# SiLU on the gate half and normalising chunk by chunk in a two-layer sequence kernel with routed experts

## What is computed

```python
scores = softmax(xt @ Wr)
topk_w, topk_idx = top_k(scores, 2)               # 8 experts, 2 for each token
topk_w = topk_w / (topk_w.sum(-1) + 1e-20)
g = silu(einsum('th,ehd->etd', xt, Wg)); u = einsum('th,ehd->etd', xt, Wu)
out = sum over the two chosen experts of topk_w * ((g * u) @ Wd)
shared = silu(x @ Sg) * (x @ Su) @ Sd
x = layernorm(x + out + shared)
```

## Time and profile before

| | |
|---|---|
| median of 3 runs | 1100.16 us (1098.81 to 1102.42) |
| the profiled execution: its own time | 1101.61 us |
| its span | 1099.7 us |
| PE, PEld (weight loads) busy | 94%, 82% |
| DVE, ACT, POOL busy | 70%, 45%, 40% |
| chain that ended last, by engine | PE 53%, DVE 19%, DVE's queue 10%, POOL 8% |
| routed experts | about 607 to 983 us of the span |
| shared expert, chunks 2 to 7, beside the gathers | about 983 to 1086 us |

### The profile page before, as it was taken

One profiled execution on the slowest core, in us unless ns is written; L12 is line 12 of the kernel. 1 busy time (PEld: TensorE's weight loads), 2 busy tenths in 40 slices (PEclk: granted clock), 3 DMA queues, 4 the chain that ended last, 5 costly groups with the idle time before them and its releaser, 6 DMA issues.

```text
span 1099.7 us, 19315 instructions
## 1 busy us (share of the span) xinstructions
PE 1032.2 (94%) x5960; PEld 901.9 (82%) x5961; DVE 764.7 (70%) x1290; ACT 489.6 (45%) x914; POOL 442.0 (40%) x445
## 2 busy tenths in 40 slices
PE   6898997799999999999999999989999999999994
PEld 5676776799999998999988787878888888888883
DVE  7988998899999987787878343333444444347886
ACT  6745755774344444666751222222322222233326
POOL 1000201555544446322100787975633200018886
PEclk9999998999999999999999999999999999999997
DMA  8100000010000000311250557464413111213335
GB/s 315 70 32 20 1 29 1 1 35 1 0 0 0 0 1 1 120 40 39 64 205 6 187 172 242 141 183 160 156 52 107 56 48 54 70 58 108 123 106 191
DMA packets 41350, 87.83 MB, mean 80 GB/s; under 512 B 5970, under 2 KB 27732, under 8 KB 39892
## 3 DMA queue, kind: packets, MB, share of 16 engines
q0 software_dynamic: 9696, 35.66, 10.5%
q1 hardware_dynamic: 20804, 39.20, 10.0%
q10 hardware_dynamic: 10800, 12.32, 3.6%
HBM read 57.80 MB, written 29.36 MB: 79 GB/s over the span
## 4 chain that ended last, share of the span: by engine, by line
PE 53%; DVE 19%; DVEq 10%; POOL 8%; issue 5%; ACT 4%; DMA 1%; ACTq 0%; POOLq 0%
PE PS L1857 14%; PE PS L1859 13%; PE PS L1858 13%; POOL gathered L1043 6%; PE PS L2260 3%; PE PS L2012 2%; DVEq L1433 2%; DVEq L1280 2%; POOL pause L1047 1%; DVEq L1447 1%; PE PS L2244 1%; DVE hx L1292 1%; PE PS L1910 1%; DVEq L1293 1%; DVE qinv L1283 1%
## 5 line engine op out<-in xcount | busy, mean ns | idle before, releaser
L1794 DVE TENSOR_TENSOR hb<-PS,gs 128x512 f32<-128x512 f32 x71 | 49.1, 692 | 154.0 <-ACT gs L784 143.4
L1043 POOL DMA_INDIRECT gathered<-expert_outputs,pos x64 | 66.7, 1043 | 139.5 <-DMA expert_outputs<-ye 127.2
L1857 PE MATMUL PS<-EWs,xeh 128*128 x284 | 119.8, 422 | 0.0
L784 ACT ACTIVATE gs<-PS 128x512 f32<-128x512 f32 x71 | 42.5, 598 | 162.3 <-PE PS L1859 154.0
L1859 PE MATMUL PS<-EWs,xel 128*128 x284 | 112.5, 396 | 0.0
L1858 PE MATMUL PS<-EWs,xeh 128*128 x284 | 111.8, 394 | 0.0
L1857 PE MATMUL PS<-WGh,bxh 128*128 128x352 f32 x256 | 88.0, 344 | 13.4 <-DVE hv L1427 10.5
L2012 PE MATMUL PS<-WD,htf 128*128 128x256 f32 x384 | 88.5, 380 | 1.6 <-ACT htf L573 1.5
L1857 PE MATMUL PS<-EWs,heh 128*128 x284 | 85.7, 302 | 3.9 <-issue 3.9
L789 ACT ACTIVATE heh<-PS 128x512 fp32r<-128x512 f32 x71 | 42.5, 598 | 104.4 <-PE PS L2260 86.9
L1798 DVE TENSOR_TENSOR hel<-PS,heh 128x512 fp32r<-128x512 f32 x71 | 49.1, 691 | 55.0 <-ACT heh L789 46.3
(11 more groups left out here) (387 smaller groups left out, 3013.5 us busy)
## 6 DMA issues: line engine op xcount, KB each, us to landing
raw_of<-experts POOLq DMA_DIRECT2D x6, 1536.0 KB
expert_outputs<-ye SPq DMA_DIRECT2D x71, 128.0 KB
xe<-tokens_by_expert ACTq DMA_DIRECT2D x65, 128.0 KB
xraw<-xT SPq DMA_DIRECT2D x8, 512.0 KB, 4.1
X<-x SPq DMA_DIRECT2D x1, 4096.0 KB, 13.3
tokens<-X SPq DMA_DIRECT2D x8, 512.0 KB, 3.1
y<-X SPq DMA_DIRECT2D x7, 512.0 KB
raw_of<-experts SPq DMA_DIRECT2D x2, 1536.0 KB, 9.5
```

Of the source, the lines that this page charges most:

```text
L784: act.activation(gs[:, h], PS[:, 2], ACT.Silu).then_inc(e_si, 1)
L1043: pool.indirect_dma_start(out=gathered[c][:, j, t], out_offset=None, in_=YS, in_offset=bass.IndirectOffsetOnAxis(ap=pos[:, j, 4 * c + t:4 ...
L1794: dve.tensor_tensor(hb[:, h], PS[:, 3], gs[:, h], ALU.mult).then_inc(e_hb, 1)
L1857: pe.matmul(out_, wh, vh, start=first, stop=False)
```

## The change

There are two edits.

In the routed experts `e_gu` is raised twice for a tile, behind the gate half and behind the up half. `silu_e` waits for the first of the two, `hidden_e` on DVE gets a wait for the second one.

At the end, the inverse deviations of chunks 0 to 4 are computed by a new DVE function, `inverse_roots(5)`, called behind `statistics(4)` at the end of unit 27 (chunk 6, quarter 3). It is a chain of 16 instructions on 128 x 20 values, each behind a drain: add epsilon; a shift and a multiply-add on the bit pattern for a first guess; four Newton steps of three instructions; minus the mean times the result. POOL's first call of `deviation4` is gone and the next one is for chunk 5 alone. ACT normalises chunks 0, 1 and 2 behind units 28, 29 and 30, and chunks 3 and 4 behind unit 31. DVE's pieces are dealt out anew: `gated(5, 3)` goes to the end of unit 27, the pieces of chunk 6 move ahead by half a unit, and the first two pieces of chunk 7 go into unit 31, ahead of `statistics(6)`.

```diff
--- before.py
+++ after.py
@@ -775,11 +775,11 @@
 
             def x_high_e(i, h):
                 act.wait_ge(e_t, i + 1)
-                wait(act, e_gu, i - 1)
+                wait(act, e_gu, 2 * i - 2)
                 act.activation(xeh[:, h].rearrange("p a c -> p (a c)"), PS[:, h, 0:D], ACT.Copy).then_inc(e_xhi, 1)
 
             def silu_e(i, h):
-                act.wait_ge(e_gu, i + 1)
+                act.wait_ge(e_gu, 2 * i + 1)
                 wait(act, e_hb, i - 1)
                 act.activation(gs[:, h], PS[:, 2], ACT.Silu).then_inc(e_si, 1)
 
@@ -819,8 +819,8 @@
             h_high_e(NE - 1, 0)
             for c in range(AHEAD, NCH - 1):
                 shared(c)
-            shared(7, chunks=((), (), ((0, 0, 4),), ((1, 0, 4),)))
-            for c in range(2, NCH - 1):
+            shared(7, chunks=(((0, 0, 4),), ((1, 0, 4),), ((2, 0, 4),), ((3, 0, 4), (4, 0, 4))))
+            for c in range(5, NCH - 1):
                 normalise(c, 0, 4)
             normalise(NCH - 1, 0, 2)
             act.wait_ge(d_rs_last, 1)
@@ -1061,17 +1061,15 @@
             pool.wait_ge(e_st1, 16 * (NE // 2))
             for c in range(NCH - 1):
                 gather(c)
-            pool.wait_ge(d_mv, 4)
-            deviation4(0, 0, 4)
             gather(NCH - 1)
             pool.wait_ge(d_mv, 6)
-            deviation4(1, 4, 6)
+            deviation4(0, 5, 6)
             pool.wait_ge(d_mv, 7)
-            deviation4(2, 6, 7)
+            deviation4(1, 6, 7)
             pool.wait_ge(d_mv, 8)
-            deviation4(3, 7, 8, slice(0, 2))
+            deviation4(2, 7, 8, slice(0, 2))
             pool.wait_ge(d_mv_last, 1)
-            deviation4(4, 7, 8, slice(2, 4), d_rs_last)
+            deviation4(3, 7, 8, slice(2, 4), d_rs_last)
 
         @block.vector
         def _(dve):
@@ -1763,6 +1761,24 @@
                     last_ = dve.bn_aggr(mv4[:, c, i], st6[:, h + i])
                 last_.then_inc(done, 1)
 
+            def inverse_roots(end):
+                varied, root, spare = mv4[:, 0:end, :, 1], rstd4[:, 0:end], nmr4[:, 0:end]
+                dve.drain()
+                dve.tensor_scalar(varied, varied, EPS, None, ALU.add)
+                dve.drain()
+                dve.tensor_scalar(spare.bitcast(U32), varied.bitcast(U32), 1, None, ALU.logical_shift_right)
+                dve.drain()
+                dve.tensor_scalar(root.bitcast(U32), spare.bitcast(U32), -1.0, float(0x5F3759DF), ALU.mult, ALU.add)
+                for _ in range(4):
+                    dve.drain()
+                    dve.tensor_tensor(spare, root, root, ALU.mult)
+                    dve.drain()
+                    dve.scalar_tensor_tensor(spare, spare, -0.5, varied, ALU.mult, ALU.mult)
+                    dve.drain()
+                    dve.scalar_tensor_tensor(root, spare, 1.5, root, ALU.add, ALU.mult)
+                dve.drain()
+                dve.scalar_tensor_tensor(spare, mv4[:, 0:end, :, 0], -1.0, root, ALU.mult, ALU.mult).then_inc(d_rs, end)
+
             def shared(c, parts=((), (), (), ()), done=((), (), (), ())):
                 for j in range(4):
                     n = 4 * c + j
@@ -1782,6 +1798,8 @@
                         x_low_late(c + 1)
                     for d in done[j]:
                         statistics(d)
+                        if d == 4:
+                            inverse_roots(5)
 
             def x_low_e(i, h):
                 dve.wait_ge(e_xhi, i + 1)
@@ -1789,6 +1807,7 @@
                                   xeh[:, h].rearrange("p a c -> p (a c)").bitcast(F32), ALU.subtract).then_inc(e_xlo, 1)
 
             def hidden_e(i, h):
+                dve.wait_ge(e_gu, 2 * i + 2)
                 dve.wait_ge(e_si, i + 1)
                 wait(dve, e_ht, i - 1)
                 dve.tensor_tensor(hb[:, h], PS[:, 3], gs[:, h], ALU.mult).then_inc(e_hb, 1)
@@ -1834,11 +1853,9 @@
             shared(3, (((0, 0),), ((0, 1),), ((0, 2),), ((0, 3), (1, 0))), ((), (), (), (0,)))
             shared(4, (((1, 1),), ((1, 2), (1, 3)), ((2, 0),), ((2, 1), (2, 2))), ((), (), (1,), ()))
             shared(5, (((2, 3),), ((3, 0), (3, 1)), ((3, 2),), ((3, 3), (4, 0))), ((2,), (), (), ()))
-            shared(6, (((4, 1), (4, 2)), ((4, 3),), ((), (5, 0)), ((5, 1), (5, 2))), ((3,), (), (), (4,)))
-            shared(7, (((), (5, 3)), ((6, 0), (6, 1)), ((6, 2), (6, 3)), ()), ((5,), (), (), (6,)))
+            shared(6, (((4, 1), (4, 2)), ((4, 3),), ((), (5, 0)), ((5, 1), (5, 2), (5, 3))), ((3,), (), (), (4,)))
             last = NCH - 1
-            gated(last, 0)
-            gated(last, 2)
+            shared(7, ((), ((6, 0), (6, 1)), ((6, 2), (6, 3)), ((last, 0), (last, 2))), ((5,), (), (), (6,)))
             added(last, (0,))
             statistics(last, range(0, 2))
             dve.wait_ge(d_gr_last, 16 * 4)
@@ -2251,7 +2268,7 @@
                     for k in range(KD):
                         at, lo = (bass.ds(base_ + i * EW + (w * KD + k) * EH, EH) for i in range(2))
                         mm = three(PS[:, 2 + w], xeh[:, h, k], xel[:, h, k], EWs[:, at], EWs[:, lo], k == 0, k == KD - 1)
-                mm.then_inc(e_gu, 1)
+                    mm.then_inc(e_gu, 1)
 
             def h_transpose_e(i, h):
                 pe.wait_ge(e_hb, i + 1)
```

## The result

| | before | changed |
|---|---|---|
| median of 8 runs each | 1100.05 us (1098.68 to 1102.42) | 1105.37 us (1102.59 to 1111.02) |
| ratio, 95% interval | | 1.0053 [1.0038, 1.0069] |
| the profiled execution: its own time, its span | 1101.61, 1099.7 us | 1111.02, 1109.1 us |
| last experts' transposes of `hb` | 977.88 us | 975.82 us |
| from there to the end of ACT's last instruction | 118.04 us | 128.34 us |

The account below looks back on a forecast made before the run. PE bounds the steady experts and ACT's backlog the end, which the change moves to DVE. The terms -0.6 + 2.2 - 0.1 = +1.5 us on the 1101.61 us execution gave a median of 1101.7 us, range 1098.0 to 1104.7.

Parts of the forecast that it names:

- The sum: Whole kernel: SiLU gain -0.6, later end +2.2, last store -0.1, together +1.5 us, for a median of 1101.7 us.
- a possible gain of the SiLU edit: Rival, experts at 660 to 740 us: earlier SiLU closes PE's gaps, 1094.8 us; chance 0.15 together with the other faster rival.
- so ACT's backlog ends the kernel: Kernel end before the change: ACT's queue of normalising tiles finishes last, DVE's chain only 1.1 to 1.3 us behind.
- +2.2 and -0.1: Tail: the end moves from ACT to DVE, 2.2 us later; the last store, finding an empty queue, lands 0.1 us quicker.
- The chain of DVE, +4.9 us at `hb` 28: Tail, ahead of unit 28: a pair of sums and the roots on DVE make `hb` of 28 end 4.9 us later.
- 4.0 us for the 16: Tail, DVE: the 16 dependent instructions for the inverse deviations take 0.25 us each, 4.0 us; bounds 2.7 to 5.5.
- PE's wait for `hb` of 28: Tail, ahead of gate-up 30: PE, needing `hb` of 28, now waits about 2.2 us.
- 13.6 forecast: Kernel end: ACT's last tile ends some 13.6 us behind the start of SiLU 31.
- The SiLU edit, -0.6 us: Routed experts: earlier SiLU shortens PE's idle wait for `hb` in the first tile, -0.6 us; bounds 0 to 1.5 us gain.
- in the steady tiles that is worth nothing: Routed experts' steady tiles: `hb` comes 0.63 us earlier but gains nothing, since PE is busy without a gap.
- The clock rival: Tail: after the new idle time the clock falls and stays low through gate-up 31, giving 1104.6 us; chance 0.15.
- the main case: The forecast itself: a short clock fall is hidden by SiLU 31, DVE's chain sets the end, 1101.7 us; chance 0.56.

Follow-up runs that it names:

- job 3: Runs on one chip beside the kernel before (1099.38 us): the change 1104.20, with pauses added 1100.70, SiLU edit alone 1097.16, that with earlier normalising 1097.34 us.
- roots, ACT's old order: The changed kernel with ACT's old normalising order (chunk 0 behind unit 30, 1 behind 31, the rest after), DVE's roots kept: 1103.44 us, ratio 1.0031.
- job 1: Runs beside the kernel before (1099.83 us), same chip as job 3: SiLU edit alone 1097.44, tail edit alone 1108.83, later first store 1104.14, ACT's old order 1103.44 us.
- SiLU, chunk 0 sooner: Kernel before plus SiLU edit, ACT normalising chunks 0, 1, 2 behind units 29, 30, 31, deviations still on POOL: 1097.34 us, ratio 0.9982 in job 3.
- pauses everywhere: The changed kernel with a small POOL instruction also behind each gather of chunks 6 and 7: 1100.70 us, ratio 1.0015 in job 3; 1089.80 us on another chip.
- job 4: Runs beside the kernel before (1087.75 us): the change 1089.75 us; with one POOL power between gathers of chunks 6 and 7, 1089.78; sixteen in a row without roots 1090.22.
- sixteen in a row without roots: Kernel before with POOL's deviations of chunks 0 to 3 moved ahead of chunk 6's gathers: 1090.22 us, ratio 1.0021 in job 4; 1089.23 us, 1.0011 in job 5.
- job 5: The three kernels of job 4 again, beside the kernel before (1087.73 us): the change 1089.70, one POOL power between gathers 1090.40, sixteen in a row without roots 1089.23 us.

## Why the prediction was wrong

**The sum left out the standstill**, the first step that failed. The prediction priced each wait by its semaphore and took the engines to run at will between them. Between 660 and 740 us the trace of before had shown that they don't: gaps ahead of PE's instructions with "issue" as their end. I read them as a possible gain of the SiLU edit and priced that rival; I did not ask whether the tail, whose gathers the change moves together, could get such a gap. It is worth 3.3 us in job 3, by the spans of the two traces, and some 6.6 us in the first profiled execution, by ACT's wait. Shown: with pauses behind the last sixteen gathers it is gone (one pair of traces, medians 3.5 us apart), it stays without the early store and with ACT's old order, and it depends on the chip. Not shown: whether the row of sixteen or the later units 28 to 31 bring it, since no chip with a standstill was had for the runs that tell these apart; nor what holds the engines. With SiLU alone the tail has none in jobs 1 and 3, nor has it one in the trace of before.

**The end was pinned to the wrong engine: "so ACT's backlog ends the kernel".** Here are five of the traces, in us, from the last experts' transposes but for the last two columns, which tell how long the span goes on behind the end of POOL's last instruction and of ACT's:

| | POOL's last | ACT's last | span | behind POOL | behind ACT |
|---|---|---|---|---|---|
| before | 116.31 | 118.04 | 121.82 | 5.51 | 3.78 |
| roots, ACT's old order (job 1) | 121.95 | 124.14 | 127.51 | 5.56 | 3.37 |
| SiLU alone (job 3) | 116.07 | 117.80 | 121.66 | 5.59 | 3.86 |
| SiLU, chunk 0 sooner (job 3) | 116.33 | 116.96 | 121.87 | 5.54 | 4.91 |
| pauses everywhere (job 3) | 119.89 | 120.52 | 125.38 | 5.49 | 4.86 |

In all twenty traces the span ends 5.49 to 5.59 us behind POOL's last multiplication, while behind ACT's last tile it is anything from 3.37 to 4.95 us. So the span follows POOL, which follows DVE's last statistics. The trace also has what fills those 5.5 us, among the instructions that are not counted as busy. Line 96 of the trace of before (count; ns, least, median, most; first and last start in us):

```profile
L96 POOLq EVENT_SEMAPHORE  x2: 17/17/17, 1099.5 to 1099.6; - x2
...
L96 POOLq DRAIN  x1: 5544/5544/5544, 1094.0 to 1094.0; - x1
...
L96 SPq DRAIN  x1: 7/7/7, 1098.6 to 1098.6; - x1
```

Line 96 is the `with` statement around the whole program, and the instructions that close the program bear its number. POOL's closing drain begins with its last multiplication and takes 5.54 us, to 1099.5; its two semaphore steps come behind it, and the span is over. SP, which has waited for the last store to land, is at the same point at 1098.6, 0.9 us sooner: that was the slack of ACT's backlog. In all twenty traces POOL's drain takes 5.54 or 5.55 us and is the last to end, even with the roots and ACT's old order, where SP comes 0.4 us ahead of it. No run was made to delay POOL or ACT by itself at the end; what POOL drains for so long is open. By the prediction's own working POOL's last instruction moves from 1094.19 to 1097.55, +3.4 us, and this should have stood in the sum for +2.2 and -0.1: -0.6 + 3.4 = +2.8 us. The rows had a hint: the transfers are over just after 1098, the span at 1099.7.

The +3.4 us can be checked without the drift ahead of unit 27. From the start of unit 27's `hb` to the end of POOL's last instruction it is 31.8 us in the trace of before and in both of SiLU alone, and 34.9 us in both traces of the change without a standstill (jobs 4 and 5): +3.1 us. DVE's `hb` and POOL's last line, before and then the change in job 4:

```profile
1062.41 0.68 DVE L1771 TENSOR_TENSOR hb<-PS,gs 128x512 f32<-128x512 f32 x1
...
1093.99 0.20 POOL L1058 TENSOR_TENSOR nmr<-nmr,rstd 128x2 f32<-128x2 f32 x1
```

```profile
1048.31 0.68 DVE L1787 TENSOR_TENSOR hb<-PS,gs 128x512 f32<-128x512 f32 x1
...
1082.99 0.20 POOL L1058 TENSOR_TENSOR nmr<-nmr,rstd 128x2 f32<-128x2 f32 x1
```

With pauses everywhere it is 35.2 us, in the change in job 3 38.4, in the first profiled execution 41.6. So in job 3: SiLU alone -2.2 us (medians), tail with pauses +3.3, together +1.1, against 1.3 measured; the standstill adds 3.3 (128.70 against 125.38 by the spans behind the transposes, 3.2 from unit 27 on): +4.4, against 4.8 measured. Medians and single traces are mixed here, and in this job they differ by up to 1.7 us for one kernel, so the closeness is partly luck. One part stays open: in the change and its variants without pauses unit 27 itself comes 84.7 to 86.4 us behind the transposes, and 83.9 to 84.6 in every trace without the roots, though the tail edit moves nothing ahead of it. On the chips of jobs 4 and 5 this is 1.4 and 1.9 us against the sixteen in a row without roots beside it, much of what the change loses there.

**The chain of DVE, +4.9 us at `hb` 28: right.** The roots take 3.82 us from the first start to the last (15 steps of 0.255 us), so 4.0 us for the 16 as forecast, not the estimated 2.8 us by the Trainium skill's page VectorE: DVE Perf Modes (its section on the TRN2 errata). Sixteen durations of 0.18 us make 2.8 us; what that estimate leaves out is the time between two of them. `hb` of unit 28 came 94.7 and 95.2 us behind the transposes in the two runs with pauses everywhere, 89.9 us before: +4.9 and +5.3. From unit 27's `hb` to unit 28's it is 5.35 us before and 10.15 in every trace of the change: +4.8. PE's wait for `hb` of 28 is 2.36 us in job 3's run with pauses (2.2 forecast):

```profile
1070.90 0.50 PE L1874 MATMUL PS<-DTh,SWh 128*128 128x512 f32 x1 [2.36 <-DVE hb L1787]
```

In the first profiled execution it is only 0.53 us. There unit 28's gate-up had waited 2.22 us for the low part of chunk 7's rows, on DVE as well, a wait that I had not followed, and behind it the granted clock was 0.50 (1.2 GHz) from 1063.2 to 1066.6: PE's work between the two waits took some 1.5 us longer and filled the second one. In job 5 the change has the same wait, 2.23 us, the clock stays at 1.00 behind it, and the wait for `hb` of 28 is 2.07 us. From SiLU 31 to the end of ACT's last tile it is 13.7 us (13.6 forecast).

**The SiLU edit, -0.6 us: right in sign, too small.** It is -2.4 and -2.2 us by the medians. The first tile gave what was said: PE's wait for `hb` fell from 1.19 to 0.57 us.

```profile
609.24 0.60 ACT L784 ACTIVATE gs<-PS 128x512 f32<-128x512 f32 x1 [2.73 <-PE PS L1876]
...
611.36 0.66 PE L2277 MATMUL PS<-C,hb 128*128 128x128 f32 x4 [0.57 <-DVE hb L1813]
```

But "in the steady tiles that is worth nothing" failed. I had looked ahead of the transposes and found 0.12 us there; the loss stood behind them. In the last five tiles, from the transposes to the next tile's first matmul, it was 0.46 us before; now it is 0.35:

```profile
966.37 0.60 PE L2277 MATMUL PS<-C,hb 128*128 128x128 f32 x4
966.72 0.48 PE L1874 MATMUL PS<-EWs,xeh 128*128 x1
```

The periods there fell from 4.92 to 4.99 us down to 4.82, the last one to 4.63; over the five that makes 0.8 us. From tile 25 to tile 65 the profiled pair gains another 0.7 us, less than 0.02 us a tile. This repeats: against the trace of before, those of SiLU alone in jobs 1 and 3 and of the change in jobs 3 and 4, on two chips, gain 0.6 to 0.8 us from tile 25 to 65 and 0.83 in the last five, and the tail alone, without the SiLU edit, neither (0.03 and 0.04 us the other way). With the first tile's half microsecond that is about 2 us. The busy share of PE could not show it: it was 60.00 of 60 us before and is 59.67 now, though the tiles became shorter. How the earlier `hb` shortens PE's way from the transposes to the gate-up was not tested.

**The clock rival: the fall came, the cost did not.** In the first profiled execution the granted clock is 0.50 from 1080.2 to 1087.1, through most of gate-up 31, as the rival had it (a row of it stands with the busy times above), but the idle time ahead of it is the standstill's. But `hb` of 30 to SiLU of 31 takes 3.22 us in this execution and 3.22 us in job 3's with pauses: DVE and ACT, not PE, set that stretch, as the main case assumed.

**A version that beats both kernels** came out: the SiLU edit alone, 1097.44 and 1097.16 us on the one chip it ran on, 7 us below the change in job 3 and 2.4 and 2.2 us below before. On the second chip, with chunks 0 to 2 normalised sooner on ACT, 1084.91 against 1087.67 us.

## What to carry to other kernels

First, find what the span's end follows by the difference of the two in several traces; the engine whose counted work finishes last need not be it, and the closing instructions of each engine are in the trace. Second, gaps whose end is "issue" or "remote" in one stage are a price that a change can bring to another: look at what POOL issued beside them, and ask whether the change makes such a place. Third, to see whether a tight loop gained, compare the starts of the same instruction from one iteration to the next, all round the loop, not the busy share, and not one of its seams alone.

## What the runs showed of the hardware

- Chips differ for one binary: the kernel before takes 1099.8 and 1099.4 us on one chip in two jobs and 1087.7 us on three others. Of the change, where both have traces, 10.6 of 13 us lie in front of the last experts' transposes (973.10 and 962.52 us), 6.0 of them between 660 and 745 us: PE is busy 77.84 of 85 us there in job 3, 83.81 in job 4.
- The span ends 5.5 us behind POOL's last counted instruction in all twenty traces, and not at a fixed distance from the last store (3.3 to 4.8 us). POOL's closing drain, 5.54 us, fills the time; that of SP takes 0.01 us.
- On one chip a standstill of several engines at once, at equal DMA share (0.64 and 0.63), with PE starting a ready matmul only every 1 to 2 us. POOL's gathers go on during it, one every 1.26 us.
- The pauses between gathers are worth 3.5 us in one place (the last sixteen, on the chip that has standstills) and cost 4.7 us in another (token gathers of the experts, net of the SiLU edit's gain), where POOL also had weights to split.
